# A routed FFN opening: weights laid out by the host, tables loaded whole, idle matmuls in the gaps

## What is computed

```python
xn = _layernorm(x, axis=-1)
s = attention(xn, Wq, Wk, Wv, Wo)          # 16 heads of 64, rotary, causal softmax
# FFN branch, xf = xn as 2048 x 1024
routing = softmax(xf @ gate_w.T)           # 8 experts
in_scale  = routing @ in_channel_scale     # 2048 x 1024
out_scale = routing @ out_channel_scale
out = (xf * in_scale) @ sign(weight).T * out_scale + bias
x = x + s * silu(out)
```

## Time and profile before

| what | value |
|---|---|
| median of 3 runs | 1185.51 us |
| profiled execution | 1189.66 us, span 1187.4 us |
| mean granted TensorE clock | 0.984 |
| TensorE busy | 1142.3 us, 96% |
| VectorE, ScalarE, GpSimd busy | 729.4, 616.2, 432.1 us |
| first FFN matmul | 49.56 us |

### The profile page before, as it was taken

One profiled execution on the slowest core, in us unless ns is written; L12 is line 12 of the kernel. 1 busy time (PEld: TensorE's weight loads), 2 busy tenths in 40 slices (PEclk: granted clock), 3 DMA queues, 4 the chain that ended last, 5 costly groups with the idle time before them and its releaser, 6 DMA issues.

```text
span 1187.4 us, 17857 instructions
## 1 busy us (share of the span) xinstructions
PE 1142.3 (96%) x5736; PEld 954.0 (80%) x5736; DVE 729.4 (61%) x1735; ACT 616.2 (52%) x1291; POOL 432.1 (36%) x258
## 2 busy tenths in 40 slices
PE   4699999999999999999999999999999998999998
PEld 3477777788888888888888888888888886888886
DVE  7676553357776777767767777767767777323133
ACT  5445344155666556656566466655665666322111
POOL 2526427433433424235333343342523523332220
PEclk9799999999999999999999999999999998999999
DMA  6734232302202022021460220202202025555652
GB/s 205 283 107 189 77 107 76 120 0 73 62 9 62 9 71 62 9 62 36 176 212 9 69 59 13 62 9 71 62 9 62 26 72 186 164 182 179 209 196 104
DMA packets 86983, 111.23 MB, mean 94 GB/s; under 512 B 3304, under 2 KB 68840, under 8 KB 85936
## 3 DMA queue, kind: packets, MB, share of 16 engines
q1 hardware_dynamic: 86960, 110.93, 28.7%
HBM read 77.37 MB, written 33.55 MB: 93 GB/s over the span
## 4 chain that ended last, share of the span: by engine, by line
PE 87%; DVE 6%; ACT 3%; POOL 2%; issue 1%; DMA 1%; SPq 0%; DVEq 0%; ACTq 0%; POOLq 0%
PE at_proj L44 17%; PE at_proj L46 17%; PE at_proj L45 17%; PE at_out L909 7%; PE at_pt L896 6%; PE ff_z_ps L264 6%; PE at_score L878 3%; PE at_score L879 3%; PE at_score L44 2%; PE at_score L45 2%; PE at_score L46 2%; PE at_proj L863 1%; POOL ff_xs_lo L601 1%; DMA w_stage<-in_L_ffn_weight_dram 1%; ACT xn_hi L365 1%
## 5 line engine op out<-in xcount | busy, mean ns | idle before, releaser
L44 PE MATMUL at_proj<-xn_hi,w_hi 128*128 128x512 f32 x896 | 363.4, 406 | 2.9 <-ACT at_v_t L1014 2.9
L46 PE MATMUL at_proj<-xn_hi,w_lo 128*128 128x512 f32 x896 | 352.0, 393 | 0.0
L45 PE MATMUL at_proj<-xn_lo,w_hi 128*128 128x512 f32 x896 | 350.8, 392 | 0.0
L46 PEld LDWEIGHTS at_proj<-xn_hi,w_lo 128*128 128x128 f32 x896 | 169.0, 189 | 37.6
L44 PEld LDWEIGHTS at_proj<-xn_hi,w_hi 128*128 128x128 f32 x896 | 169.5, 189 | 33.3 <-issue 3.3
L45 PEld LDWEIGHTS at_proj<-xn_lo,w_hi 128*128 128x128 f32 x896 | 169.8, 190 | 30.4
L1273 POOL TENSOR_TENSOR at_turning<-at_turning,rope_table 128x512 f32<-128x512 f32 x64 | 82.9, 1296 | 305.1 <-DVE at_turning L1144 305.1
L1281 POOL TENSOR_TENSOR w_lo<-w_stage,w_hi 128x1024 fp32r<-128x1024 f32 x45 | 114.5, 2559 | 162.8 <-ACT w_hi L993 162.8
L1031 ACT ACTIVATE at_prob<-at_score,at_neg_max 128x512 f32<-128x512 f32 (+3 forms) x256 | 133.4, 526 | 68.0 <-DVE at_neg_max L1172 67.6
L1040 ACT ACTIVATE at_pt_hi<-at_pt 128x512 fp32r<-128x512 f32 (+1 forms) x192 | 94.0, 524 | 101.1 <-PE at_pt L896 100.4
L1189 DVE TENSOR_TENSOR at_pt_lo<-at_pt,at_pt_hi 128x512 fp32r<-128x512 f32 (+1 forms) x192 | 111.8, 597 | 43.7 <-ACT at_pt_hi L1040 42.8
(11 more groups left out here) (129 smaller groups left out, 1827.7 us busy)
## 6 DMA issues: line engine op xcount, KB each, us to landing
z_store<-z SPq DMA_DIRECT2D x16, 512.0 KB, 2.7
w_stage<-in_L_attn_Wq_dram SPq DMA_DIRECT2D x16, 512.0 KB, 3.8
w_stage<-in_L_attn_Wk_dram SPq DMA_DIRECT2D x16, 512.0 KB, 5.1
w_stage<-in_L_attn_Wv_dram SPq DMA_DIRECT2D x16, 512.0 KB, 6.1
att_store<-at_att_t SPq DMA_DIRECT2D x32, 256.0 KB, 2.0
rope_table<-att_store SPq DMA_DIRECT2D x16, 512.0 KB, 6.5
z<-_attn_hidden_states_dram SPq DMA_DIRECT2D x16, 512.0 KB, 4.5
at_turning<-z_store SPq DMA_DIRECT2D x16, 512.0 KB, 6.1
```

Of the source, the lines that this page charges most:

```text
L44: pe.matmul(out, sh, mh, start=first, stop=False)
L45: pe.matmul(out, sh, ml, start=False, stop=False)
L46: return pe.matmul(out, sl, mh, start=False, stop=final)
```

## The change

- The host hands over the weight transposed (`weight_t`), the gate table as 128 x 64 (`gate_t`), and each channel table already repeated in four groups of 32 rows with zeros between. All layout, no arithmetic.
- Each of the eight weight tiles has its own buffer, in memory that the second batch's high and low parts use later; no load of them waits. ScalarE takes the sign straight into the matmul's operand.
- The channel tables' low parts move from GpSimd to VectorE, one instruction of 64 x 1024 each (rows 64 to 127). The gate of batch 0 is done in two halves of 256 tokens. The router is otherwise one round for each batch, as before.
- TensorE does 6, 4, 3 and 6 matmuls of no use (`warm`) at four places of the opening.
- x tiles 4 and 5 go to other buffers. The order of batch 0 is new on TensorE, ScalarE, VectorE and GpSimd; batches 1 to 3 keep theirs.

The diff, cut to its core:

```diff
-        X_SLOT = (0, 1, 2, 5, 0, 1, 2, 5, 3, 4, 0, 1, 2, 5, 3, 4)
+        X_SLOT = (0, 1, 2, 5, 3, 4, 0, 1, 2, 5, 3, 4, 0, 1, 2, 5)
+        X_BANKS = {1: 1, 2: 0, 3: 1}
...
             load(0)
             load(1)
-            load_rows(0)
+            sp.dma_start(gate_raw[:].rearrange("p k e -> p (k e)"), io["gate_t"]).then_inc(gate_in, 16)
             load(2)
             load(3)
+            load_rows(0)
+            load_table(0)
             load_rows(1)
...
             load_rows(2)
-            load_rows(3)
+            load_table(1)
+            for t in range(3, KT):
+                load_rows(t)
             load(4)
             load(5)
...
+            def warm(count):
+                for _ in range(count):
+                    pe.matmul(osc_ps[:], keep["ident_r"][:], keep["ident_r"][:].unsqueeze(1).to_broadcast([P, QT, P]),
+                              start=True, stop=True)
...
-            pe.wait_ge(ident_copies, 2)
-            sign_transposes(0)
+            pe.wait_ge(ident_copies, 1)
             x_transposes(0)
-            sign_transposes(1)
             x_transposes(1)
-            gate_w_transposes()
+            warm(WARM[0])
             x_transposes(2)
             x_transposes(3)
-            sign_transposes(2)
+            warm(WARM[1])
             pe.wait_ge(tables, 1)
-            gate(0)
-            sign_transposes(3)
+            gate(0, (0, 1))
+            gate(0, (2, 3))
+            warm(WARM[2])
             gate_transposes(0)
-            sign_transposes(4)
-            sign_transposes(5)
+            warm(WARM[3])
             route_transposes(0)
...
+            pe.wait_ge(chan_lo, 1)
+            for k in range(4):
+                in_scale(0, k)
+            pe.wait_ge(chan_lo, 2)
+            for k in range(KT):
+                ffn(0, (k,))
+                if k + 4 < KT:
+                    in_scale(0, k + 4)
+            ffn(1, range(KT))
             for j in range(BATCH):
...
+                if j == 0:
                     x_transposes(m)
+                    ffn(2, range(1))
                     x_transposes(m + 1)
+                    ffn(2, range(1, 4))
                     x_transposes(m + 2)
+                    ffn(2, range(4, 6))
                     x_transposes(m + 3)
+                    ffn(2, range(6, KT))
+                    gate(1)
+                    ffn(3, range(2))
+                    gate_transposes(1)
+                    ffn(3, range(2, 4))
...
         def _(act):
             def sign(t):
...
+                act.wait_ge(w_in[t], 16)
+                act.activation(keep["sign_t"][:, t, :], weight_row(t), ACT.Sign).then_inc(signed, 1)
...
+            gate_w_high()
+            ln_root(0, 2)
+            x_high(0)
+            ln_root(1, 2)
+            x_high(1)
+            chan_high(0)
+            sign(0)
+            x_high(2)
+            x_high(3)
+            sign(1)
+            sign(2)
+            sign(3)
+            gate_copy(0)
+            parts_copy(0)
+            route_exp(0)
+            sign(4)
+            chan_high(1)
+            route_copy(0)
+            xs_high(0, range(1))
+            xs_high(0, range(1, 2))
+            out_scale(0, 0)
+            sign(5)
+            xs_high(0, range(2, 3))
+            sign(6)
+            xs_high(0, range(3, 4))
+            sign(7)
+            xs_high(0, range(4, KT))
+            ln_root(2, 2)
+            out_scale(0, 1)
+            out_scale(1, 0)
+            out_scale(1, 1)
...
+                if j == 0:
+                    x_high(m)
+                    out_scale(2, 0)
+                    x_high(m + 1)
+                    ln_root(3, 2)
+                    out_scale(2, 1)
+                    x_high(m + 2)
+                    x_high(m + 3)
+                    ln_root(4, 2)
+                    gate_copy(1)
+                    out_scale(3, 0)
+                    parts_copy(1)
+                    route_exp(1)
+                    out_scale(3, 1)
+                    route_copy(1)
+                    xs_high(1, range(4))
...
         @block.vector
...
+            def chan_low(c):
+                table = keep[("chan_in", "chan_out")[c]]
+                dve.wait_ge(chan_hi, c + 1)
+                dve.tensor_tensor(table[64:P, :], chan_rows[64:P, c, :], raw(table[64:P, :]), ALU.subtract).then_inc(chan_lo, 1)
...
             layer_norm(0)
+            gate_w_low()
             layer_norm(2)
             x_low(0)
             x_low(1)
-            sign_copy(1)
-            gate_w_low()
             x_low(2)
+            chan_low(0)
             x_low(3)
-            layer_norm(4)
-            sign_copy(3)
             router(0)
             scale(0, range(2))
-            sign_copy(5)
-            sign_copy(7)
+            chan_low(1)
             scale(0, range(2, 4))
+            ln_stats(4, 2)
+            scale(0, range(4, KT))
+            ln_finish(4, 2)
+            z_scale(0)
...
+                if j == 0:
+                    x_low(m)
+                    z_scale(1)
+                    layer_norm(m + 2)
+                    x_low(m + 1)
+                    x_low(m + 2)
+                    x_low(m + 3)
+                    z_scale(2)
+                    layer_norm(m + 4)
+                    router(1)
+                    scale(1, range(4))
+                    z_scale(3)
...
         @block.gpsimd
...
-            chan_low(0)
-            chan_low(1)
-            xs_low(0, range(4))
+            xs_low(0, range(KT))
             pool.wait_ge(bias_in, 16)
+            z_bias(0)
+            z_bias(1)
+            z_bias(2)
+            xs_low(1, range(4))
```

More of the change, by code:

```diff
@@ L46, in split_matmuls, with round_of @@
     return pe.matmul(out, sl, mh, start=False, stop=final)
+ROUNDS = tuple((j, 0, QT) for j in range(BATCH))
+def round_of(tile):
+    return tile // QT
 def ffn_block(nc, block, io, keep, xn, xn_store, z_store):
@@ L178, in _ @@
                 if j == BATCH - 1:
-                    sp.wait_ge(xs_l, BATCH * KT)
+                    for k in range(2):
+                        wait_xs_low(sp, len(ROUNDS) - 1, KT - 2 + k)
                     sp.dma_start(keep["rope"][:], io["rope"].rearrange("c p n -> p c n")).then_inc(keep["rope_in"], 16)
@@ L187, in _ @@
         def _(pe):
[L188 to L200, removed]
             def x_transposes(n):
@@ L214, in x_transposes, with gate, gate_transposes @@
                     last.then_inc(x_tr, 1)
[L216 to L220, removed]
-                for k in range(KT):
[L222 to L227, removed]
+            def gate(r, tiles=range(QT)):
+                hi, lo = xn[r % 2]
+                cols = slice(tiles[0] * P, (tiles[-1] + 1) * P)
+                pe.wait_ge(x_lo, 2 * (QT * r + tiles[-1] + 1))
+                if r >= 1:
+                    pe.wait_ge(route_sb, r)
+                for k in range(KT):
+                    pe.matmul(small_ps[0:2 * EXPERTS, cols], keep["gate_t"][:, k, :], hi[:, k, cols], start=(k == 0), stop=False)
+                    last = pe.matmul(small_ps[0:2 * EXPERTS, cols], keep["gate_t"][:, k, :], lo[:, k, cols],
+                                     start=False, stop=(k == KT - 1))
+                if tiles[-1] == QT - 1:
+                    last.then_inc(gate_mm, 1)
+            def gate_transposes(r):
+                pe.wait_ge(gate_sb, 2 * r + 1)
                 for t in range(QT):
@@ L530, in router @@
                 else:
                     dve.wait_ge(route_zero, 1)
-                dve.tensor_copy(route4[:, :, 0:EXPERTS], route[:])
-                then(dve.tensor_copy(route4[:, :, 32:32 + EXPERTS], route[:]))
-                for c in (64, 96):
-                    dve.tensor_tensor(route4[:, :, c:c + EXPERTS], route[:], raw(route4[:, :, 0:EXPERTS]),
+                dve.tensor_copy(route4[:, 0:count, 0:EXPERTS], rt)
+                then(dve.tensor_copy(route4[:, 0:count, 64:64 + EXPERTS], rt))
@@ L1364, in build @@
             keep["rope_in"], keep["z_add"], keep["xn_ok"] = sem("rope_in"), sem("z_add"), sem("xn_ok")
-            xn = [[sb(with_xn, f"xn{b}_{part}", [P, KT, SEQ], F32R) for part in ("hi", "lo")] for b in range(2)]
+            xn = [[sb(with_xn, f"xn0_{part}", [P, KT, SEQ], F32R) for part in ("hi", "lo")]]
+            with ExitStack() as opening:
+                keep["weight_rows"] = sb(opening, "weight_rows", [P, KT, EMBED], F32)
+            xn.append([sb(with_xn, f"xn1_{part}", [P, KT, SEQ], F32R) for part in ("hi", "lo")])
             with ExitStack() as with_ffn:
@@ L1398 @@
     for name in _INS:
[L1399 removed]
+        a = laid_out(name, inputs[name])
         arrays[f"in_{name}_dram"] = a
```

360 lines of the change are left out of this document (177 added, 183 removed).

## The result

The changed kernel takes 1184.56 us, the median of 15 runs, where the kernel before took 1186.76 in 15: ratio 0.998, 95% interval 0.9972 to 0.9988. By that ratio it is faster by 2.4 us (1.4 to 3.3) and not by 6.0. The profiled execution took 1184.56 us (span 1182.8, mean granted clock 0.991).

The account below looks back on a forecast made before the run. TensorE, busy 96% of the span, bounds the kernel; other engines set the opening. Tile 0 14.5 us earlier, less 5.3 idle and later waits, leaves 6.0: 1183.7 profiled, 1179.5 us median, range 1172 to 1186.

Parts of the forecast that it names:

- rival A: Opening gained, then a new stall in batch 0 before x_transposes(6): 1179.5 us, by itself 1176.5 to 1182.5; chance 0.60.
- the fifth product: Fifth in-scale product of batch 1, closing batch 0 on TensorE: forecast at 88.2 us in place of 94.2.
- Part 1 and 2: Opening, from weights and gate to logits: first x_low 3.3 us earlier, at 15.9; logits at 24.3 us, before 31.5.
- Part 2: Opening, up to the logits: the idle matmuls priced at 0, bounds 0 and 1; high clock taken for the second gate half.
- Rival C: Opening gains little through late transfers or low clock: tile 0 done 9.5 us earlier, gain 1.0, 1184.5 us; chance 0.20.
- Part 3: Router of batch 0: VectorE's stall goes, first x scaling at 30.4 us, 6.1 us from the logits in place of 11.5.
- Part 4: First tile of batch 0: scaling and low parts, tile 0 done at 46.3 us against 60.8, 14.5 earlier; bounds 44.4 and 49.
- Part 5, the stall: Batch 0 before x_transposes(6): VectorE's 10.2 us chain no longer covered, start at 65.0 us, 5.3 us idle.
- Part 5, behind the stall: From x_transposes(6) to batch 1's fifth in-scale product: 1.2 us for slower matmuls, gate at 73.2, product at 88.2 us.
- The change is worth what it moves that point: After batch 1's fifth in-scale product both kernels have the same instruction order, so nothing counted there; total gain 6.0 us.
- B: Batch 0 before x_transposes(6): the stall is hidden and nearly all of the 14.5 us stays, 1172 us; chance 0.12.
- D: Batch 0 from x_transposes(6): the clock falls and waits keep it low until 94 us; 11 us extra, 1190; chance 0.08.

Follow-up runs that it names:

- e3: The changed kernel without its 19 idle matmuls (all four counts 0): 1185.29 us, ratio 0.9988 to the kernel before.
- e2: The changed kernel with VectorE's layer norm of tiles 6 and 7 directly behind z_scale(0), its Sqrt behind out_scale(1, 1): 1180.54 us, ratio 0.9951 to the kernel before.
- e5: The changed kernel with every FFN SBUF tensor at its address in the kernel before, order unchanged: ratio 0.9961 to the kernel before, FFN matmul median 389 ns.
- f_pad160: The changed kernel with 160 unused bytes per partition ahead of the router's buffers: one run, FFN matmul median 389 ns, no ratio given.
- e7: The changed kernel with only the opening reordered (gate table copy, channel low parts, Signs, statistics of tiles 4 and 5): 1180.40 us, ratio 0.9941 to the kernel before.

## Why the prediction was off

The mechanism of rival A was right, its size was not: 6.0 us forecast, 2.4 measured. Of the 3.6 us missing, 1.1 had been lost when x_transposes(6) started, 1.4 between it and the fifth product, and 1.1 behind that product, where I had counted nothing. By its steps:

- *Part 1 and 2*, logits at 24.3: 24.6. Right. I had not priced that the gate table's copy, with a second table load behind it, now stands ahead of the first Sqrt. In the profiled run both were over when the Sqrt's input was ready; in e3's, where the gate table came later, VectorE waited 1.6 us longer for the Sqrt.
- *Part 2*, idle matmuls at no cost: right. That they hold the high clock for the gate: true for its first six matmuls, since without them (e3) only these ran at half pace, some 0.6 us. Rival C's 3.6 us for this is six times that.
- *Part 3*: no VectorE operation on 128x2 numbers over 0.17 us before 37, right; the stall of the earlier trace rows is gone. Scaling at 30.68, forecast 30.4. The terms written there for the way to the Exp add up to 26.9, not the 27.2 that was used; by the trace it was done at 27.6.
- *Part 4*: low parts end at 34.3, 35.6, 37.5, 39.0, 41.9, 43.2, 44.7, 46.0 by the trace. I had 33.1 and 34.4 for the first two: I let VectorE wait for GpSimd, and it was GpSimd that waited. Tile 0 at 47.2 for 46.3. The rule of the Trainium skill (SBUF — State Buffer, section "SBUF: two separate sides") that the prediction cites agrees: VectorE started 0.22 us ahead of GpSimd, and GpSimd's pair took 0.86 us longer than the 2.52 it takes alone. My order of the two was wrong.
- *Part 5, the stall*: x_transposes(6) at 66.1 for 65.0, all of the 1.1 brought in from tiles 0 and 1; the chain from the end of x_transposes(4) took 10.3 us for 10.2. Idle 4.05 for 5.3 (the terms written there give 10.2 - 4.7 = 5.5), in part because x_transposes(5) also waited for VectorE, 0.7 us that I had left out. Right in place and cause; e2 removed it and got its price back.
- *Part 5, behind the stall*: this step failed in size, 24.6 us from x_transposes(6) to the fifth product for 23.2. To the gate it was 9.0 for 8.2, from the gate to the route transposes 9.5 for 9.1, from there to the product 6.1 for 5.9. It is not the half-clock stretch, which was right at 1.2: without it (e2) the three legs are 7.8, 9.5 and 6.1, where my terms had 7.0, 9.1 and 5.9. In the second leg z_scale(2) and the norm of tiles 8 and 9 took 6.8 us together (74.96 to 81.78), where the prediction wrote 5.8. How the rest divides over the interlocked waits, which I had priced one by one, stays open.
- *"The change is worth what it moves that point"*: failed. From the point on the order is the same, as stated, but the FFN matmuls of the batches behind it cost 1.1 us more, because dropping `ident_bf` and adding buffers had moved their operands (e5, f_pad160). The prediction had put everything behind the product at nothing.

Rival A was the case, though its own range of 1176.5 to 1182.5 was missed. The median of 1184.56 us is the number of rival C (1184.5), by chance: C had tile 0 done 9.5 us earlier, and it was 13.6. B was not reached by e2 alone (0.9951, where 1172 would be 0.989). D did not happen: the clock was back before 75.

## What to carry to other kernels

A shorter opening can leave another engine's next chain uncovered. Here VectorE's norm of tiles 6 and 7 had been hidden under 9.5 us of TensorE work, and in the new order too little was left above it. So list what each wait of the shortened stretch hides, look for idle time of that engine further ahead, and move the chain there in the same edit. Two instructions that hold each other up should not be placed side by side only because one engine happens to be free: the 1.2 us subtraction found 3.5 us of free VectorE time six to nine us earlier, once ScalarE had rounded the table in time (e7). When small buffers come or go, compare the median duration of the big matmuls before and after, and not the order alone: a few bytes made 512 of them 2% longer.

## What the runs showed of the hardware that was not expected

- Matmuls of 512 float32 columns took 389 ns when stationary and moving operand lay a multiple of 256 bytes apart in a partition, 393 at 128 over it, 395 at 32 over, 397 at 96 over. From start to start of two it was 0.454 and 0.468 us at the ends.
- A VectorE subtraction of two SBUF inputs (64x1024, 1.22 us) that started 0.2 us ahead of a GpSimd one delayed it by 0.86 us; in the kernel before it was VectorE that stood, 1.87 us for an operation of 0.16.
- After the same 4.05 us without work, TensorE's next eight transposes ran at half pace in the changed kernel (1.94 us) and at full pace in e7_opening (1.19 us), where the half pace began only behind them.
- The gate table's 32 KB, third in SyncE's queue, let ScalarE start at 5.79 us in one execution and at 7.25 in another, although VectorE could start on x tile 0, ahead of it in the queue, at 4.16 and 4.04.
